# Expert blocks' attention: the causal mask of the diagonal block is added by VectorE instead of by a product on TensorE

## The reference, cut to what matters

```python
def _attention(h, wq, bq, wk, bk, wv, bv, wo, bo):      # H = 16 heads, HD = 128, b = 2, s = 512
    q = (h @ wq + bq).reshape(b, s, H, HD).transpose(0, 2, 1, 3)
    ...
    q = q * cos + _rotate_half(q) * sin
    k = k * cos + _rotate_half(k) * sin
    scores = jnp.einsum('bhqd,bhkd->bhqk', q, k) / math.sqrt(HD)
    causal = jnp.tril(jnp.ones((s, s), bool))
    scores = jnp.where(causal[None, None], scores, jnp.finfo(jnp.float32).min)
    probs = jax.nn.softmax(scores.astype(jnp.float32), axis=-1).astype(q.dtype)
    out = jnp.einsum('bhqk,bhkd->bhqd', probs, v)
```

## Time and profile before

| | us |
|---|---|
| median of 3 runs (lowest, highest) | 2605.76 (2604.42, 2606.11) |
| the profiled execution | 2609.29 |
| its span, first to last instruction | 2607.4 |
| busy in the span: PE | 2329.5 (89%) |
| busy in the span: DVE | 1677.2 (64%) |
| busy in the span: ACT | 1191.4 (46%) |
| busy in the span: POOL | 1100.7 (42%) |
| mask products L1532, 256 of them, each | 0.219 |

### The profile page before, as it was taken

The page is one execution under the profiler, slowest core; times in us unless marked ns, Lnnn a source line. Parts: engine busy times, 40 slices in busy tenths (PEclk is TensorE's granted clock), DMA queues, the critical chain, the costliest instruction groups (busy, mean ns, idle before and its releaser), DMA issues. The chain is left out here.

```text
span 2607.4 us, 49048 instructions
## 1 busy us (share of the span) xinstructions
PE 2329.5 (89%) x18400; PEld 1615.0 (62%) x18400; DVE 1677.2 (64%) x3286; ACT 1191.4 (46%) x2936; POOL 1100.7 (42%) x1265
## 2 busy tenths in 40 slices
PE   7888888888888888888759999999889989999999
PEld 4577655776557865577635666676533356666685
DVE  7667686677766767677536777742357567777613
ACT  5655455554555545555324555432115535455411
POOL 0477434774347743377525544420130035444300
PEclk9999999999999999999879999998889989999999
DMA  2100001000010000000012000000100030000000
GB/s 63 37 2 3 2 17 37 2 2 2 17 37 2 2 2 17 17 3 2 2 52 74 15 19 19 7 1 1 50 1 1 1 115 19 19 19 13 1 1 17
DMA packets 57640, 46.29 MB, mean 18 GB/s; under 512 B 11576, under 2 KB 50880, under 8 KB 57024
## 3 DMA queue, kind: packets, MB, share of 16 engines
q1 hardware_dynamic: 57408, 43.16, 5.7%
HBM read 42.10 MB, written 1.05 MB: 17 GB/s over the span
## 5 line engine op out<-in xcount | busy, mean ns | idle before, releaser
L1182 DVE SCALAR_TENSOR_TENSOR work<-four,taps,work 128x511 f32<-128x511 f32 (+2 forms) x384 | 285.4, 748 | 101.6 <-ACT work L861 92.0
L1807 POOL TENSOR_TENSOR rot<-q_plain,ropes 128x512 f32<-128x512 f32 x64 | 81.0, 1266 | 577.0 <-ACT q_plain L1838 577.0
L931 ACT ACTIVATE work<-four 128x512 f32<-128x512 f32 x216 | 129.0, 597 | 270.1 <-PE four L690 243.8
L576 PE MATMUL four<-xT,wring 128*128 128x512 f32 x512 | 252.2, 620 | 0.2 <-DVE work L1182 0.2
L741 PE MATMUL four<-work 128*128 128x128 f32 x1536 | 217.2, 286 | 0.0
L1851 ACT ACTIVATE pr<-four,nmaxf 128x512 f32<-128x512 f32 (+3 forms) x256 | 134.0, 525 | 171.2 <-DVE nmaxf L1689 171.2
L1689 DVE TENSOR_REDUCE nmaxf<-four 128x1 f32<-128x512 f32 (+3 forms) x256 | 125.8, 491 | 125.7 <-PE four L1532 121.7
L741 PEld LDWEIGHTS four<-work 128*128 128x128 f32 x1536 | 193.5, 196 | 4.0
L1530 PE MATMUL four<-rot,rot 128*128 128x512 f32 (+3 forms) x512 | 179.0, 445 | 5.2 <-DVE rot L1681 3.6
L1117 POOL TENSOR_TENSOR work<-work 128x256 f32<-128x256 f32 x184 | 146.5, 796 | 77.5 <-DVE work L1263 56.1
L1124 POOL TENSOR_TENSOR work<-work 128x256 f32<-128x256 f32 x184 | 141.9, 771 | 84.0 <-PE bank L775 74.0
(11 more groups left out here) (276 smaller groups left out, 5429.3 us busy)
## 6 DMA issues: line engine op xcount, KB each, us to landing
wqkv<-in_f_wq_dram SPq DMA_DIRECT2D x32, 128.0 KB, 2.2
wqkv<-in_f_wk_dram SPq DMA_DIRECT2D x32, 128.0 KB, 2.4
wqkv<-in_f_wv_dram SPq DMA_DIRECT2D x32, 128.0 KB, 2.3
wo<-in_f_wo_dram SPq DMA_DIRECT2D x2, 2048.0 KB, 11.7
we<-in_f_we_dram SPq DMA_DIRECT2D x4, 1024.0 KB
wring<-in_Wk_dram SPq DMA_DIRECT2D x4, 512.0 KB, 3.8
wring<-in_Ww_dram SPq DMA_DIRECT2D x4, 512.0 KB, 5.5
wring<-in_Wv_dram SPq DMA_DIRECT2D x4, 512.0 KB, 3.9
```

The lines of the kernel that those rows point to most:

```text
L576: last = nc.tensor.matmul(unit_bank(i)[:], wring[n % 2][:, c, h * P:(h + 1) * P], k.xT[:, c, b * T:(b + 1) * T], start=(c == 0), stop=(c = ...
L1182: ins = nc.vector.scalar_tensor_tensor(out=cbuf[i % 4][:, n:], in0=unit_bank(i)[:, 0:T - n], scalar=taps[:, {"q": 0, "k": 1}.get(kind, 2), ...
```

## The change

DVE adds the f32 mask, which already lies in SBUF as `causal`, to the diagonal block of the scores in place in PSUM, ahead of the maximum, and waits for that addition. PE's mask product, the bf16 copies of the identity and the mask, and the semaphore `masks_in` go. The score product itself now raises `s_made`. The new semaphore `s_masked` orders DVE's maximum behind its addition.

```diff
                     nc.tensor.matmul(k.bank[2 + i % 2][:, 0:(qt + 1) * P], q[:, qt * P:(qt + 1) * P],
-                                     kk[:, 0:(qt + 1) * P], start=True, stop=False)
-                    nc.tensor.matmul(k.bank[2 + i % 2][:, qt * P:(qt + 1) * P], eye_b[:], causal_b[:],
-                                     start=False, stop=True).then_inc(s_made, 1)
+                                     kk[:, 0:(qt + 1) * P], start=True, stop=True).then_inc(s_made, 1)
...
-                pe.wait_ge(masks_in, 2)
                 for u in range(UNITS_B):
...
                     dve.wait_ge(s_made, i + 1)
                     if i >= CH:
                         dve.wait_ge(s_exp, i - CH + 1)
+                    diagonal = k.bank[2 + i % 2][:, qt * P:(qt + 1) * P]
+                    nc.vector.tensor_tensor(diagonal, diagonal, causal[:], ALU.add).then_inc(s_masked, 1)
+                    dve.wait_ge(s_masked, i + 1)
                     nc.vector.tensor_reduce(nmax[:, n:n + 1], k.bank[2 + i % 2][:, 0:(qt + 1) * P], AX.X, ALU.max,
                                             negate=True).then_inc(s_max, 1)
...
-                nc.vector.tensor_copy(eye_b[:], k.eye[:]).then_inc(masks_in, 1)
-                nc.vector.tensor_copy(causal_b[:], causal[:]).then_inc(masks_in, 1)
                 rope_k(0)
```

More of the change, by code:

```diff
@@ L1424, in expert_block @@
             nmax, rs = tb("nmaxf", [P, CH]), tb("rs", [P, CH])
-            eye_b, causal_b = tb("eye_b", [P, P], BF16), tb("causal_b", [P, P], BF16)
         raw, gap, comb = sb("raw", [P, NT, E]), sb("gap", [P, NT, E]), sb("comb", [P, NT, E])
@@ L1445, in expert_block @@
         o_made, o_kept = sem("o_made"), sem("o_kept")
-        masks_in = sem("masks_in")
+        s_masked = sem("s_masked")
         out_made, h_added, x_joined = sem("out_made"), sem("h_added"), sem("x_joined")
```

## The result

The changed kernel takes 2615.3 us (median of 9 runs, 2610.1 to 2622.2), the kernel before in the same comparison 2605.5 (9 runs, 2596.8 to 2607.5). The ratio is 1.0047, 95% interval 1.0032 to 1.0062: slower by 0.5%, or 12 us (8 to 16); the two medians alone differ by 9.8. The profiled execution of the changed kernel took 2622.2 us, its span is 2620.4, against 2609.3 and 2607.4 before. Lines that follow the removed ones have moved up by one to four: L1807 of POOL before is L1804 now, L1810 is L1807, L1813 is L1810 and L1823 is L1820; of DVE L1681 is L1677, L1689 is L1688 and L1697 is L1696; L1530 and L1543 of PE are L1529 and L1540 now. L1686 is the new addition.

The account below looks back on a forecast made before the run. The prediction took a loop through q_plain, POOL's query rotation, L1681 and the last scaling as the bound. 46 x 0.12 + 16 x 0.38 = 11.6 us on 2605.8 gave 2617.4, range 2610 to 2624.

Parts of the forecast that it names:

- The bound: Expert-block attention: a loop through q_plain, POOL's query rotation, L1681 and the last scaling sets the 11.14 us unit period.
- PE is the bound: Rival for the attention units: PE sets the time, so 64 x 0.41 = 26 us is gained, 2580; chance 0.02.
- The mask products: On PE, each costs 0.06 plus 0.06 us; the first two shorten the loop by 0.23, all four free some 0.41.
- The addition: Four 128x128 mask additions in PSUM on DVE per unit, 0.28 us each, plus 0.035 for each wait.
- The race: DVE's third scaling starts 0.04 us after POOL's first L1810, loses, and ends at 1539.71, behind L1810's end at 1539.56.
- The plain units: 46 units without POOL's L1823: period 11.25 or 11.26 us, +0.12 each.
- The bias units: 16 units where POOL's L1823 starts 0.13 us ahead of L1681 and wins: period 11.6, +0.38 each.
- The sum: Over the expert-block units, 46 x 0.12 + 16 x 0.38 = 5.5 + 6.1 = 11.6 us slower.
- Rival 1: DVE's third scaling wins against POOL: 62 x 0.08 to 0.23 = 5 to 14 us faster, 2592 to 2601; chance 0.24.
- Rival 2: Third scaling loses to POOL in the 16 units with L1823, wins in the others: about 0, 2603 to 2609; chance 0.08.

Follow-up runs that it names:

- the reordering: Fourth maximum (with its addition, where present) moved ahead of the third row's scaling on DVE: changed kernel 2590.4 us, same order in the kernel before 2603.1 us.
- the last pair: Changed kernel and kernel before, both with the key rotation's cosine product kept in PSUM and third and fourth scalings behind the rotation: 2576.8 and 2585.1 us.
- The run with 96 columns: Changed kernel with each mask addition covering only the first 96 of the diagonal block's 128 columns: 2619.5 us, one run.
- 64 columns: Changed kernel with each mask addition covering only 64 of the diagonal block's 128 columns: 2596.6 us, one run.

## Why the prediction was right

It forecast 2617.4 for a median of 2605.8, +11.6; measured was +12 by the ratio.

- **The bound.** The loop through q_plain, POOL's rotation, L1681 and the last scaling: right. In the kernel before that scaling ends 0.22 ahead of the next scores, the same distance as in the changed kernel, where PE is seen to wait for it. POOL started 0.22 earlier in the unit (4.32 us after the unit's first scores, 4.55 before), for 0.23 forecast. "PE is the bound" was wrong for this pair of kernels, as the reordering showed, but not far off: the run without a mask reached it.
- **The mask products**, 0.12 each and 0.41 for four: right in size. Without products and additions PE needs 10.63, and with the products, in the last pair, 11.03: 0.40.
- **The addition**, 0.28 from a row that writes SBUF: 0.291 in PSUM, with 0.035 for the wait. By the row of the Trainium skill's table for a PSUM source and an SBUF destination ("VectorE: DVE Perf Modes", "The TRN2 errata") the estimate would have been 0.258; the measurement is 0.033 above it, and 0.013 above the row of this program that the forecast took.
- **The race.** Start of the third scaling forecast at 5.70 after the unit's first scores, measured 5.75; 0.04 behind POOL forecast, 0.08 measured. Its length 1.33 and its end 0.15 behind POOL: as forecast. The run with 96 columns shows that even 0.02 ahead would have lost, so the forecast was less of a coin toss than it looked: 0.033 off each addition did not turn it, 0.066 did.
- **The plain units**: +0.12 forecast, +0.13 measured. **The bias units**: +0.38 forecast, +0.44 measured, because L1820 takes 0.72 when it is not held up, and not 0.6 to 0.7. That estimate took the wait off the blocked length (1.06 less 0.47), but left out the 0.15 between its start and the moment at which POOL takes hold, which the prediction itself uses for the race; with it the sum is 0.74.
- **The sum**: 11.6 forecast, 12.3 in the stretches, 13.1 by the medians.
- Rival 1 (DVE wins the race) is what 64 columns gave, 11.01, or 0.12 less than before, inside its 0.08 to 0.23. Rival 2 (a race that goes both ways) did not come here; its mechanism, the 0.07 by which POOL is earlier in the bias units, decided in the run without a mask.

What the prediction lacked is the third race. In the kernel before, L1681 starts 0.12 behind L1813 and loses. An edit that brings it to L1813's start takes POOL out of the loop, and then all of PE's saving counts, as in the plain units of the run without a mask.

## What to carry to other kernels

Where two engines share something that is held for a whole instruction, the price of an added instruction is not its length: it is a step, set by who arrives first at the next contested one. Before an edit that shifts one of them by some 0.3 us, write down the distance between the starts of each pair that competes, and ask which pairs change sides. In the two stretches the same edit was worth +12 us as it was made, -15 us with two lines swapped on DVE in both kernels, and -14 and -11 us in the two pairs in which the last addition of the key rotation no longer competes with POOL.

## What the runs showed of the hardware that I had not expected

- A two-input addition on DVE and a two-input POOL instruction that start together are decided within some nanoseconds. Of the pairs like the earlier trace rows in the slot attention of the kernel before, 20 start within 0.01 of each other, DVE always 3 to 8 ns behind: it wins in ten of them (3 to 6 ns behind) and loses in ten (5 to 8 ns). In the expert blocks without a mask it wins 0.05 ahead and loses 0.02 behind. A scaling with one input needs a lead: it loses 0.02 ahead and wins 0.05 ahead.
- The one that loses is not slowed, it is blocked: 0.35 became 1.43, 0.69 became 1.70, and POOL's 1.27 became 1.78.
- An addition in place in PSUM with the second input in SBUF takes 0.291 us for 128x128, whether POOL is running or not.
